# First attention of a transformer layer: the score matmuls of a step put in crossed order with its matmuls for row maxima

## The reference

```python
q = q * cos + _rotate_half(q) * sin
k = k * cos + _rotate_half(k) * sin
attn = jnp.einsum('bhqd,bhkd->bhqk', q, k) * SCALE
alibi = diff[None, :, :] * slopes[:, None, None] * MAX_BIAS   # diff = min(key - query, 0)
attn = attn + alibi[None]
w = jax.nn.softmax(attn, axis=-1)
out = jnp.einsum('bhqk,bhkd->bhqd', w, v)
```

## Time and profile before

| | us |
|---|---|
| median of three executions | 1895.72 (1887.87 to 1905.27) |
| the profiled execution, its time | 1900.91 |
| the profiled execution, its span | 1899.1 |
| TensorE busy | 1641.6 |
| VectorE busy | 1301.5 |
| ScalarE busy | 993.5 |
| windows of the first attention with maxima (15), each | 47.7 |

### The profile page before, as it was taken

One profiled execution on the slowest core, in us unless ns is written; L12 is line 12 of the kernel. 1 busy time (PEld: TensorE's weight loads), 2 busy tenths in 40 slices (PEclk: granted clock), 3 DMA queues, 4 the chain that ended last, 5 costly groups with the idle time before them and its releaser, 6 DMA issues. The chain is left out here.

```text
span 1899.1 us, 36270 instructions
## 1 busy us (share of the span) xinstructions
PE 1641.6 (86%) x14816; PEld 1072.0 (56%) x14816; DVE 1301.5 (69%) x2288; ACT 993.5 (52%) x1692; POOL 402.9 (21%) x268
## 2 busy tenths in 40 slices
PE   7948999999999999999585798868993999999970
PEld 6824444444444444444374555546763888889870
DVE  6777888888888888885295537752333677777736
ACT  5323777777777777778443257853442333333310
POOL 6540000000000000000223101111551344444440
PEclk9956999999999999999797659988996999999995
DMA  7878444545444444420555847313213233333225
GB/s 253 196 185 235 60 67 61 70 64 68 66 63 67 69 64 68 62 35 9 178 174 169 117 73 121 76 56 131 91 39 108 67 92 93 92 93 93 37 33 178
DMA packets 131421, 183.98 MB, mean 97 GB/s; under 512 B 30918, under 2 KB 95572, under 8 KB 130200
## 3 DMA queue, kind: packets, MB, share of 16 engines
q1 hardware_dynamic: 117816, 159.60, 39.5%
q0 software_dynamic: 13440, 22.07, 5.4%
HBM read 114.99 MB, written 69.99 MB: 97 GB/s over the span
## 5 line engine op out<-in xcount | busy, mean ns | idle before, releaser
L661 DVE TENSOR_REDUCE att_row_max<-att_ring 128x2 f32<-128x1024 f32 x512 | 602.3, 1220 | 108.8 <-PE att_ring L727 57.1
L645 ACT ACTIVATE att_w_exp<-att_s_ps 128x512 f32<-128x512 f32 x999 | 536.2, 599 | 222.9 <-PE att_s_ps L774 150.8
L801 PE MATMUL att_a_ps<-att_w_exp,att_v_group 128*32 128x512 f32 x2048 | 273.6, 606 | 0.8 <-ACT att_acc_sb L634 0.6
L760 PE MATMUL att_s_ps<-att_q_stack,att_k_stack 62*128 62x512 f32 x640 | 182.0, 481 | 0.0
L760 PEld LDWEIGHTS att_s_ps<-att_q_stack,att_k_stack 62*128 62x128 f32 x640 | 84.4, 184 | 124.0 <-ACT att_w_exp L645 112.9
L2193 ACT ACTIVATE ex_hid<-ex_h_ps,ex_b 128x512 f32<-128x512 f32 x128 | 87.2, 686 | 117.6 <-DVE ex_h_lo L2248 64.0
L2149 POOL DMA_INDIRECT x_scr<-ex_y,ex_home x64 | 106.4, 1662 | 181.8 <-DVE ex_y L2238 167.2
L583 POOL COPY att_eyes<-keep_slope_eye 128x384 bf16<-128x384 bf16 x16 | 8.1, 510 | 641.8 <-PE att_s_ps L774 632.5
L2248 DVE TENSOR_TENSOR ex_h_lo<-ex_hid,ex_h_hi 128x512 fp32r<-128x512 f32 x128 | 138.7, 1084 | 4.4
L727 PE MATMUL att_ring<-att_k_stack,att_q_stack 60*128 60x512 f32 x640 | 131.5, 451 | 6.2 <-DVE att_att L688 3.2
L774 PE MATMUL att_s_ps<-att_eyes,keep_past_bf 64*128 64x64 bf16 x3738 | 130.6, 193 | 0.0
(11 more groups left out here) (296 smaller groups left out, 3601.8 us busy)
## 6 DMA issues: line engine op xcount, KB each, us to landing
first_w_raw<-ew SPq DMA_DIRECT2D x16, 1024.0 KB, 7.6
att_k_stack<-qk_scr SPq DMA_DIRECT2D x120, 128.0 KB
cr_q_stack<-q_scr SPq DMA_DIRECT2D x48, 256.0 KB, 9.2
keep_k_stack<-qk_scr SPq DMA_DIRECT2D x72, 128.0 KB
rows_scr<-att_zeros POOLq DMA_DIRECT2D x8, 1040.0 KB, 22.4
ex_rows<-rows_scr SPq DMA_DIRECT2D x16, 520.0 KB, 4.7
att_q_stack<-qk_scr SPq DMA_DIRECT2D x60, 128.0 KB
qk_scr<-qkv_t_hi SPq DMA_DIRECT2D x7, 1024.0 KB, 4.3
```

What stands on the lines that cost most here:

```text
L645: nc.scalar.activation(w_exp[(STEPS * g.n + st) % SETS][h][:, :], score_bank(v), ACT.Exp).then_inc(exp_done, 1)
L661: nc.vector.tensor_reduce(out, ring[place.slot][:, :, :], AX.X, ALU.max).then_inc(ring_free, 1)
L760: ins = nc.tensor.matmul(score_bank(v), ks[g.buf][rows, c, j, kt * P:(kt + 1) * P], qs[g.buf][rows, j, c * CH:(c + 1) * CH], start=True, s ...
L801: ins = nc.tensor.matmul(a_ps[32 * h:32 * h + 32, :], vg[g.buf][:, kt, h * VW:h * VW + 32], w_exp[(STEPS * g.n + st) % SETS][h][:, :], sta ...
```

## The change

The scores of a step are no longer written as pairs with their biases at once. In a window with maxima the order becomes: values and transposes as before; S2, then (a wait for the ring) U0b, U0a, S3, then the biases of S2 and S3, then those of U0; then, in the new `next_scores`, S0', (a wait for the ring) U1b, U1a, S1', the biases of U1, then those of S0' and S1'. So the first score of each pair is followed by the unit's matmul of the other half of the array's rows, and so on. `max_pair` is only split in two, and stays in use before the first window. The scores S0 and S1 of step 0 of a window are issued at the end of the window before; for the first window they stand ahead of it. In the last window the order of the matmuls is what it was. The wait for the new maxima (`top_in`) goes with S0'.

```diff
+            def score_biases(g, st, h):
+                for n in range(12):
+                    for i in range(2):
+                        score_bias(g, st, h + i, n)
...
+            def next_scores(g, st, m, u):
...
+                new = g if st + 1 < STEPS else g.plus(1)
+                at = (st + 1) % STEPS
+                if at % KT == 0:
+                    pe.wait_ge(top_in[at // KT], 32 * new.n + 32)
+                if m is None:
+                    score_pair(new, at, 0)
+                    return
+                place = PLACES[g.n, "max", u]
+                score_main(new, at, 0)
+                pe.wait_ge(ring_free, place.need)
+                max_main(m, u, 1, place)
+                ins = max_main(m, u, 0, place)
+                score_main(new, at, 1)
+                max_biases(m, u, place, ins)
+                score_biases(new, at, 0)
...
                 for st in range(STEPS):
-                    c, kt = divmod(st, KT)
-                    if kt == 0:
-                        pe.wait_ge(top_in[c], 32 * g.n + 32)
-                    score_pair(g, st, 0)
...
-                    score_pair(g, st, 2)
                     if with_max:
-                        for i in range(2):
-                            max_pair(n, 2 * st + i, PLACES[g.n, "max", 2 * st + i])
-
+
+                        place = PLACES[g.n, "max", 2 * st]
+                        score_main(g, st, 2)
+                        pe.wait_ge(ring_free, place.need)
+                        max_main(n, 2 * st, 1, place)
+                        ins = max_main(n, 2 * st, 0, place)
+                        score_main(g, st, 3)
+                        score_biases(g, st, 2)
+                        max_biases(n, 2 * st, place, ins)
+                        next_scores(g, st, n, 2 * st + 1)
+                    else:
+                        score_pair(g, st, 2)
+                        if st + 1 < STEPS:
+                            next_scores(g, st, None, None)
+
+            pe.wait_ge(top_in[0], 32)
+            score_pair(g0, 0, 0)
             windows(window)
```

More of the change, by code:

```diff
@@ L738, in max_pair @@
             def max_pair(g, u, place):
-                half, j, q, kk = max_unit(u)
                 pe.wait_ge(ring_free, place.need)
@@ L742, in max_pair, with max_biases @@
                     ins = max_main(g, u, i, place)
+                max_biases(g, u, place, ins)
+            def max_biases(g, u, place, ins):
+                half, j, q, kk = max_unit(u)
                 if kk == half:
@@ L781, in score_pair @@
                     score_main(g, st, h + i)
-                for n in range(12):
-                    for i in range(2):
-                        score_bias(g, st, h + i, n)
+                score_biases(g, st, h)
+            def next_scores(g, st, m, u):
[14 more added lines that the diff above has]
+                score_biases(new, at, 0)
             def transpose_top(g, half, place):
```

## The result

The changed kernel takes 1927.13 us (median of 4, 1924.09 to 1929.18), the kernel before beside it 1900.49 (median of 4, 1887.87 to 1909.70). The ratio is 1.016, with an interval of 1.012 to 1.020: slower, as forecast. By the medians it is 26.6 us more, where 38 were forecast (1934 us).

A forecast was written before the change was run, and what follows sets the result against it. The prediction took a chain of latencies through ScalarE as the bound, not any engine's work. Terms 1.92 + 0.48 + 0.15 = 2.55 us a window, times 15 windows, gave 38 us more: 1934 us on the median, range 1913 to 1956.

The forecast's parts named there:

- The bound: Window steps: loop S2, its exponential, S1', values, next S2 sums to 2.60 us without score biases, 3.00 with them.
- S2 and its biases: In 8 steps with score biases, U0a ahead of S2's biases delays S2's exponential by 0.24: 1.92 us a window.
- S3, S0', U1 between S0' and S1': S3 0.34 later, S0' earlier, U1's matmuls while S1' waits for its bank: nothing lost or won.
- Biases of U1: Behind S1', on the loop: 0.06 in steps 8, 12, 13, 14, 0.12 in 11 and 15, 0.48 us a window.
- Steps 9 and 10: Step 9: U0 to values 1.21 instead of 1.06, plus 0.15; step 10: both engines equally later, counted 0.
- The ring in step 1: Wait for the ring before U0b, with S2's biases behind it, would hold S2's exponential in steps 1 and 2; counted 0.
- Loads saved: Rival: mains behind mains save some 0.1 us each if TensorE's order ends last, 36 us faster, 1865; chance 0.06.
- Absorbed: Rival: unseen slack takes up the exponential's 0.24, leaving U1's biases and step 9, 9.5 us, 1905 median; chance 0.08.
- No running side by side: Rival: S2 and U0b don't overlap, S1' 0.6 to 0.75 later in all steps, 160 us, some 2060; chance 0.04.
- Maxima too late: Rival: U1 finished some 0.9 us later in steps 8 to 15, VectorE holds the ring, 36 us more, 1970; chance 0.08.

The follow-up runs named there:

- the three pushes: U0a's matmul issued twice (changed kernel): 1972.18 us; maxima's biases left out (kernel before): 1889.53; S2's exponential over 384 of 512 columns (kernel before): 1881.74.
- u0_crossed_only: Changed kernel with U1, S0' and S1' back in the old order, only S2, U0b, U0a, S3 crossed: 1926.24 us, 1.017 of the kernel before.
- u1_crossed_only: Changed kernel with S2, S3 and U0 back in the old order, only S0', U1b, U1a, S1' crossed: 1898.66 us, 1.0003 of the kernel before.
- s2_biases_first: Changed kernel with S2's biases issued ahead of U0a and S3's right behind S3: 1.004 of the time of the kernel before.
- both_first: Changed kernel with S2's biases ahead of U0a and U1's biases ahead of S1', all crossings kept: 1.003 of the time of the kernel before.
- biases_before_wait: Changed kernel with U1's biases ahead of S1' and S2's biases ahead of the wait for the ring and U0b: 1924.18 us in its one run.
- u1_biases_first: Changed kernel with U1's biases issued ahead of S1' instead of behind it: 1.009 of the time of the kernel before.

## Why the prediction was right, and where it was off

**The bound.** Right. That S1' starts 0.05 after S2's exponential, the sums 2.60 and 3.00 and the independence from the units carried the case; the three pushes confirm it from both sides. TensorE busy for 47.09 of 47.71 us would have led the other way.

**S2 and its biases.** Forecast 0.24 in 8 steps, 1.92 a window, and the exponential 0.97 after S2. Measured by `u0_crossed_only`: 0.23 to 0.25 in each, 1.90 a window; the exponential of step 0 starts at +0.97 in the median of 12 windows of the changed kernel. U0a's load behind S2 was hidden: step 0 grew by 0.23, not by a stream and a load. In the rows of step 0 above, the loads of U0b and U0a lie between 414.02 and 414.31, inside S2's record (414.02 to 414.51), and S2's record is of U0a's own half. So the rule of the Trainium skill (TensorE: Matmul & The Clock Gate, "The mechanism"), by which U0a's load would have been exposed, does not hold here either, and the 0.1 a step that the prediction put on it did not come. The same section also says that a load may be pulled ahead into the background weight buffer, and that fits the trace.

**S3, S0', U1 between S0' and S1'.** Counted at nothing, and steps 4 to 7 with 2.60 to 2.61 bear it out.

**Biases of U1.** Forecast 0.06, and 0.12 in steps 11 and 15. `u1_crossed_only` shows 0.08, 0.12, 0.05, 0.07, 0.06 and 0.12 in steps 8 and 11 to 15.

**Steps 9 and 10.** This is the term that was mis-sized. Forecast for steps 8 to 10: 0.06 + 0.15 + 0 = 0.21 more. Measured: 0.08 + 0.08 - 0.22 = 0.06 less, 0.27 a window and 4 us in all. The path within step 9 was right, as the changed kernel's rows show, from U0 to the values 1.21:

```profile
392.04 0.50 PE L727 MATMUL att_ring<-att_k_stack,att_q_stack 60*128 60x512 f32 x2 [0.25 <-DVE att_row_max L661]
...
393.25 0.16 PEld L826 LDWEIGHTS att_a_ps<-att_w_exp,att_v_group 128*32 128x32 f32 x8
```

What failed is "TensorE and VectorE both come later by the same time". VectorE did not come later: U0b and U0a start together when the ring is released, since S2 is done by then, and the reduction starts 0.54 behind, as before (384.64 to 385.19). Nor did it come later in step 10. These are the first reductions of steps 9 and 10, of the kernel before and then of the changed one:

```profile
385.19 1.23 DVE L661 TENSOR_REDUCE att_row_max<-att_ring 128x2 f32<-128x1024 f32 x1 [0.41 <-PE att_ring L727]
...
388.28 1.22 DVE L661 TENSOR_REDUCE att_row_max<-att_ring 128x2 f32<-128x1024 f32 x1
...
392.58 2.36 DVE L661 TENSOR_REDUCE att_row_max<-att_ring 128x2 f32<-128x1024 f32 x2 [0.41 <-PE att_ring L727]
...
395.68 1.22 DVE L661 TENSOR_REDUCE att_row_max<-att_ring 128x2 f32<-128x1024 f32 x1
```

Both pairs lie 3.09 to 3.10 apart. Only the values moved. So what step 9 loses, step 10, which waits for VectorE, gives back. Whoever finds one engine bound in a stretch has to sum the stretch on that engine. The rest of the difference to the forecast is small: 2.21 a window for 2.55, 33 us in the windows for 38. That the spans differ by 27.1 only is the chance of the stretches outside the windows.

**The ring in step 1.** Counted at nothing, and it cost nothing, but by luck. The slot came free 0.02 us before S2 started, in part because the change itself draws step 0 out. In `s2_biases_first` and `both_first` the same wait costs step 1 0.29 us.

**The rivals.** "Loads saved" fell with steps 4 to 7, which got no shorter; `biases_before_wait` shows its condition (S1' not waiting) met in all steps with score biases, and that kernel is slower. "Absorbed" fell with 0.23 in all 8 steps. "No running side by side" fell with S2 and U0b both at 414.02. "Maxima too late" was not met in the changed kernel, where U1 finished earlier takes only 0.05 to 0.11 off steps 12 to 15 (`u1_biases_first`); a wait for VectorE turned up where the rival did not look for it, in step 1 of `both_first`.

## What to carry to other kernels

Before an order is changed, find the loop: which instruction ends each wait in a step, what releases that, and whether the legs sum to the period in two kinds of step. Then only instructions put between two legs cost, each by its own time, and work between the waits is free to move and gains nothing. That holds as long as the loop ends last: `both_first` and `biases_before_wait` put no matmul between two legs and still lost 0.6 and 1.7 us a window against the kernel before, to the wait for a ring slot and to TensorE's own order. Where two engines alternate as the bound, cheap service work (merging, copies, transposes) belongs into the steps in which the engine that does it has idle time; here that brought 0.4%.

## What the runs showed of the hardware

A half of the array can be starved by the order alone. In `both_first` the 12 biases of S2 in step 14 delay S3 in the other half, although U0b ahead of it had streamed. The last two rows are S2's exponential, with that of S3, and S1':

```profile
398.33 0.50 PE L727 MATMUL att_ring<-att_k_stack,att_q_stack 60*128 60x512 f32 x1
...
398.67 0.47 PE L777 MATMUL att_s_ps<-att_eyes,keep_past_bf 64*128 64x64 bf16 x10
...
398.95 0.50 PE L763 MATMUL att_s_ps<-att_q_stack,att_k_stack 62*128 62x512 f32 x1
...
399.03 0.48 PE L727 MATMUL att_ring<-att_k_stack,att_q_stack 60*128 60x512 f32 x1
...
399.23 1.22 ACT L645 ACTIVATE att_w_exp<-att_s_ps 128x512 f32<-128x512 f32 x2 [0.72 <-PE att_s_ps L777]
...
400.05 0.48 PE L763 MATMUL att_s_ps<-att_q_stack,att_k_stack 62*128 62x512 f32 x1
```

In the changed kernel S3 follows U0b by 0.34 (414.02 and 414.36); here that would be 398.67. It starts at 398.95, when 10 of S2's 12 biases have started. It also starts 0.08 before U0a (399.03), which stands ahead of it in the program but behind S2's biases in the low half: matmuls of different halves can start in another order than that of the program. Two matmuls of different halves that stand together start together, but a run of small ones for one half holds what stands behind it for the other; how far TensorE looks ahead I did not measure by itself. With 6 biases in the same place steps 0, 3, 12 and 13 are back at what they were before, so there the delay stayed off the loop. Step 15 is not (3.08 instead of 2.99).
